# Products of the scan states with C for three of four chunks on GpSimd, sums and gates of the finished chunk three steps later

## What is computed

```python
def _L0_attn_ref(u, in_proj_w, dt_projs_weight, dt_projs_bias, x_proj_w, A, D, norm_B_w, norm_C_w, out_proj_w):
    xz = u @ in_proj_w.T
    x, z = jnp.split(xz, 2, axis=-1)
    x = jax.nn.silu(x)
    dt = jax.nn.softplus(x @ dt_projs_weight.T + dt_projs_bias)
    BCp = (x @ x_proj_w.T).reshape(Bsz, L, NHEADS, -1)
    ...
    Bc = jax.lax.complex(Bn[..., 0], Bn[..., 1])
    Cc = jax.lax.complex(Cn[..., 0], Cn[..., 1])
    ...
    zt = Ac[None, None] * (0.5 * dt)[..., None]
    den = 1.0 - zt
    abar = (1.0 + zt) / den
    u_in = Bc * ((dt * x_sum)[..., None] / den)
    def step(h, inp):
        a, b = inp
        h = a * h + b
        return (h, h)
    _, hs = jax.lax.scan(step, h0, (jnp.swapaxes(abar, 0, 1), jnp.swapaxes(u_in, 0, 1)))
    y_red = jnp.real(Cc * hs).sum(axis=-1)
    y = (xh * (y_red + D)[..., None]).reshape(Bsz, L, D_INNER)
    y = y * jax.nn.silu(z)
    return y @ out_proj_w.T
```

## Time and profile before

| | |
|---|---|
| median of 3 runs | 1005.39 us (1004.13 to 1006.34) |
| the profiled execution | 1000.66 us |
| its span, first to last instruction | 998.3 us |
| mean granted TensorE clock | 0.919 of full speed |
| PE busy | 814.4 us (82%) |
| DVE busy | 737.3 us (74%) |
| ACT busy | 560.7 us (56%) |
| POOL busy | 200.5 us (20%) |
| scan on VectorE, first to last step | 290.6 to 534.7 us |

### The profile page before, as it was taken

One profiled execution on the slowest core, in us unless ns is written; L12 is line 12 of the kernel. 1 busy time (PEld: TensorE's weight loads), 2 busy tenths in 40 slices (PEclk: granted clock), 3 DMA queues, 4 the chain that ended last, 5 costly groups with the idle time before them and its releaser, 6 DMA issues. The chain is left out here.

```text
span 998.3 us, 26552 instructions
## 1 busy us (share of the span) xinstructions
PE 814.4 (82%) x9663; PEld 482.8 (48%) x9663; DVE 737.3 (74%) x2440; ACT 560.7 (56%) x1410; POOL 200.5 (20%) x216
## 2 busy tenths in 40 slices
PE   4899999998865788696683387796996999999787
PEld 2577777775322233242231264564665555555453
DVE  5688888885589999999996885456563666666667
ACT  3689888988674658566240576454433333333345
POOL 1477666764000000000000011002110000000037
PEclk9999999999997788998796698998797999999979
DMA  7111111100000000000000702100570000000001
GB/s 247 34 45 40 42 37 42 37 16 3 1 0 1 1 0 1 1 1 0 1 0 1 177 2 98 75 4 3 197 298 14 1 1 0 0 0 0 2 9 34
DMA packets 23415, 36.56 MB, mean 37 GB/s; under 512 B 5668, under 2 KB 19748, under 8 KB 21156
## 3 DMA queue, kind: packets, MB, share of 16 engines
q1 hardware_dynamic: 23336, 35.53, 11.3%
HBM read 34.48 MB, written 1.05 MB: 36 GB/s over the span
## 5 line engine op out<-in xcount | busy, mean ns | idle before, releaser
L442 ACT ACTIVATE xa_prob<-xa_s,xa_nmax 128x257 f32<-128x257 f32 x256 | 128.1, 503 | 21.0 <-DVE xa_nmax L579 19.3
L726 POOL TENSOR_TENSOR xa_prob<-xa_prob,xa_rinv 128x1028 f32<-128x1028 f32 x64 | 121.5, 1900 | 76.7 <-DVE xa_rinv L586 75.7
L579 DVE CUSTOM_DVE_ANT_0 xa_s<-xa_s_ps,xa_nbias 128x257 f32<-128x257 f32 x256 | 93.2, 420 | 12.3 <-ACT xa_prob L442 6.4
L1637 POOL TENSOR_TENSOR mo_disp_t<-mo_disp_t,mo_rst 128x256 f32<-128x256 f32 x16 | 9.8, 615 | 362.3 <-DVE mo_rst L1616 362.3
L2262 PEld LDWEIGHTS ca_z_ps<-ca_xn_t,ca_m_t 128*128 128x128 f32 x512 | 62.1, 199 | 30.5 <-issue 25.9
L2345 ACT COPY ca_z<-ca_z_ps 128x512 f32<-128x512 f32 x64 | 37.5, 585 | 69.0 <-PE ca_z_ps L2262 69.0
L272 PE MATMUL xa_t_ps<-identity,xa_prob 128*128 128x128 f32 x512 | 69.5, 279 | 4.1 <-ACT xa_p_t L451 1.8
L2262 PE MATMUL ca_z_ps<-ca_xn_t,ca_m_t 128*128 128x128 f32 x512 | 67.9, 288 | 4.0 <-ACT ca_xn_t L2339 3.9
L569 DVE COPY xa_kvs<-xa_kv_ps 128x512 f32<-128x512 f32 x64 | 44.1, 689 | 34.3 <-PE xa_kv_ps L246 34.3
L272 PEld LDWEIGHTS xa_t_ps<-identity,xa_prob 128*128 128x128 f32 x512 | 54.8, 141 | 25.6 <-issue 25.6
L451 ACT COPY xa_p_t<-xa_t_ps 128x1024 f32<-128x1024 f32 x64 | 63.4, 991 | 2.2 <-PE xa_t_ps L272 2.2
(11 more groups left out here) (353 smaller groups left out, 1912.6 us busy)
## 6 DMA issues: line engine op xcount, KB each, us to landing
xa_ctx_t<-in_ctx_t SPq DMA_DIRECT2D x64, 128.5 KB, 2.1
room<-in_ctx_t SPq DMA_DIRECT2D x8, 1028.0 KB, 6.5
room<-in_ctx_n SPq DMA_DIRECT2D x8, 1024.0 KB, 4.8
ss_wx<-in_ss_wx SPq DMA_DIRECT2D x1, 2048.0 KB, 7.9
xres<-in_x SPq DMA_DIRECT2D x4, 256.0 KB, 5.3
out_x<-xres SPq DMA_DIRECT2D x4, 256.0 KB, 2.3
ma_mask_u<-in_mask SPq DMA_DIRECT2D x4, 128.5 KB
room<-in_ca_wk SPq DMA_DIRECT2D x1, 512.0 KB, 3.5
```

The source lines that it names most:

```text
L442: nc.scalar.activation(prob[:, r, g, :], s_sb[:, b, g, :], ACT.Exp, bias=nmax[:, r, g:g + 1], scale=-1.0, accum_out=rsum[:, r, g:g + 1]).t ...
L579: nc.vector.tensor_tensor_reduce(out=s_sb[:, b, g, :], in0=s_ps[:, g, 0:S], in1=nbias[:, g, :], scale=1.0, scalar=3e38, op0=ALU.add, op1=A ...
L726: nc.gpsimd.tensor_tensor(prob[:, r, :, :], prob[:, r, :, :], bc(rinv[:, r, :].rearrange("p (g o) -> p g o", o=1), (P, G, S)), ALU.mult).t ...
```

## The change

For chunks 0, 1 and 2 the four products of the states with C are taken from VectorE's table and given to GpSimd, as a block of its own with the same operands. The first product of a chunk waits until the last step of the chunk is done, each waits for its C planes, and nothing stands between them. The products of chunk 3 stay on VectorE. `scaled_y`, `gated_y`, `residual`, the row statistics, the moments and (in chunks 1 and 2) the decay work move later: from (6,1) to (9,1), from 8 and 9 to 11 and 12, from 13 to 16, from 14 and 18 to 17 and 21, and from 14, 16, 19, 21 to 16, 18, 21, 23. `step_size` and `input_size` move earlier, from step 9 to step 7. On TensorE `reduce_y(c - 1)` goes behind `step_sizes(c + 1)`.

```diff
@@ state_space, tensor @@
-                if c >= 1:
-                    reduce_y(c - 1)
                 if more:
                     step_sizes(c + 1)
                 if c >= 1:
+                    reduce_y(c - 1)
                     spread_y(c - 1)
@@ state_space, vector, fill(c, l, gap) @@
-                if before and gap < 2 and 1 <= l < 3:
-                    outputs(c - 1, 2 * (l - 1) + gap)
...
-                if before and at == (6, 1):
+                if before and at == (9, 1):
                     scaled_y(c - 1)
-                if before and gap == 1 and l in (8, 9):
-                    gated_y(c - 1, l - 8)
-                if after and at == (9, 0):
+                if before and gap == 1 and l in (11, 12):
+                    gated_y(c - 1, l - 11)
+                if after and at == (7, 0):
                     step_size(c + 1)
-                if after and at == (9, 2):
+                if after and at == (7, 2):
                     input_size(c + 1)
-                if before and at == (13, 1):
+                if before and at == (16, 1):
                     residual(c - 1)
...
-                first = (14, 16, 19, 21) if before else (18, 20, 23, 25)
+                first = (16, 18, 21, 23) if before else (18, 20, 23, 25)
@@ state_space, new @@
+        @block.gpsimd
+        def _(pool):
+            def outputs(c, h):
+                if h == 0:
+                    pool.wait_ge(step_done, (5 * N - 1) * (c + 1))
+                pool.wait_ge(c_ready, 8 * c + 2 * h + 2)
+                nc.gpsimd.tensor_tensor(w[:, c % 2, :, h, :], w[:, c % 2, :, h, :], c_pl[:, :, h, :], ALU.mult).then_inc(prod_ready, 1)
+
+            for c in range(CH - 1):
+                for h in range(H):
+                    outputs(c, h)
```

8 lines of the change are left out of this document (4 added, 4 removed).

## The result

The new kernel takes 1020.39 us (median of 4 runs, 1018.49 to 1021.37) against 1004.76 us of the kernel before on the same chip (4 runs, 1000.13 to 1006.34). The ratio is 1.016 [1.012, 1.020]. The forecast was 1019.8 us. Run a second time later, the new kernel had 1.0185 [1.0151, 1.0218].

What follows compares the result with a forecast made beforehand. VectorE was taken to bound the scan, busy 63.03 of 66.20 us in chunk 1. 24.6 us of standstill, less 12.1 of products and 1.7 of old waits, plus 3.6 of newton waits, gave +14.4 us: 1019.8 us, range 1009 to 1028 us.

Steps and rivals of the forecast that it cites:

- GpSimd's product: Duration of one 1024-element product on GpSimd, 2.35 us from its other rows; four take 9.4 us.
- The standstill: VectorE's scan instructions held by GpSimd's products at the start of chunks 1 to 3: 8.2 us each, 24.6 us together.
- The products taken off VectorE: Four products fewer in each of three chunks, 1.01 us each: 4.04 us a chunk, 12.1 us saved.
- the old waits: VectorE's waits at L1236 just ahead of (9,0) go: 1.10 us in chunk 1, 0.6 us in chunk 2.
- The step size: In (7,0) VectorE arrives 2.1 us after the softplus and does not wait; undisturbed it would wait 6.1 us in chunk 1.
- The newton: In (16,0) VectorE waits 1.8 us in chunks 1 and 2, as spread_y runs at TensorE's lower clock after idleness.
- The scan in all: Sum over chunks 1 to 3: 24.6 us less 12.1 and 1.7 us, plus 3.6 us, +14.4 us.
- Chunk 0 and all later stages keep their length: Sign to check: everything outside chunks 1 to 3, the work behind the scan included, stays unchanged in length.
- no standstill: Rival: GpSimd's reads go beside the scan's without holding VectorE; 1003.2 us, or 1006.8 us with newton waits; 8%.
- the partial one: Rival: GpSimd gives way while running, VectorE loses 3 to 5.5 us per chunk; 1007.2 to 1010.8 us; 15%.
- the heavier one: Rival: VectorE's instructions lengthen GpSimd's or get in less often, 11 us per chunk; 1028 us; 11%.

Runs made afterwards that it cites:

- other tiles: Kernel before, products on VectorE, plus four unused 1024-element GpSimd TENSOR_TENSORs at the start of chunks 1 to 3 on tiles of their own: 1019.7 us, ratio 1.016.
- quarters: Changed kernel with each GpSimd product cut into four pieces, sixteen for a chunk: 1017.31 us, ratio 1.017.
- the kernel with TensorE kept busy: Changed kernel with seven extra 512-column matmuls, result overwritten, ahead of spread_y's wait on TensorE: 1010.81 us, ratio 1.011.
- the seven matmuls: Changed kernel with seven extra matmuls ahead of spread_y's wait, 512 columns wide (1010.81 us, ratio 1.011) or one column wide (1013.1 us, ratio 1.011).
- thirteen short matmuls: Kernel before with gates one step later and thirteen one-column matmuls ahead of the last reduce_y's wait for the products: 993.6 us, ratio 0.991.
- Kept busy ahead: Kernel before with gates one step later and thirteen 512-column matmuls ahead of the last reduce_y's wait for the products: 994.7 us, ratio 0.994.
- the moves only: Changed kernel with its twelve products put back on VectorE at (1,0) to (2,1), all other moves kept: 1006.3 us, ratio 1.004.
- GpSimd only: Kernel before with only the products of chunks 0 to 2 given to GpSimd, all else in its old place: 1012.86 us, ratio 1.009.

## Why the prediction was right, point by point

The median came out 0.6 us above the forecast. The scan did what the forecast says, for the reasons that it gives. One stage that was to keep its length grew, and the fit of the totals is partly luck.

- **GpSimd's product**, taken from the slope of its rows as 2.35 us: 2.355 to 2.401 us. Right.
- **The standstill**, 8.2 us for a chunk by the rule "one VectorE instruction gets in for each GpSimd instruction": 8.36 us. Right, and the mechanism was shown twice more: with other tiles (it follows GpSimd's reads, not the data) and with quarters (it follows the number of pieces). One row that the forecast leaned on is of another kind: L2082 is a TENSOR_SCALAR with one large input, and no run here tests that kind.
- **The products taken off VectorE**, 1.01 us each, and the old waits, 1.7 us. Chunk 3, with nothing else in it, came out +4.3 against 8.2 - 4.04 = +4.2 us. In the changed kernel all waits at L1235 are behind the scan, so the 1.7 us went as written. On their own they would not have gone in full: with the gates one step later only 1.0 us came off, since the step size was late next. The standstill covers that too.
- **The step size** in (7,0) waits for nothing. Right, and right for the given reason: without the standstill it waits 2.8 us in the two chunks together.
- **The newton**, 1.8 us in each of chunks 1 and 2 from a TensorE at its lower clock: 1.38 and 1.62 us. L948 took 3.78 us where I had 3.48. Shown by the kernel with TensorE kept busy: its two waits vanish and chunks 1 and 2 are 1.7 and 2.1 us shorter.
- **The scan in all**: +14.4 us forecast, +14.6 us measured, chunk by chunk 4.9, 5.4, 4.2 against 4.7, 5.6, 4.3. The 0.2 us are closer than the parts: the standstill was 0.5 us too low in all and the newton 0.6 us too high, and the second trace of the new kernel has +13.8 us.
- **"Chunk 0 and all later stages keep their length"** is the step that failed. The tail grew by 3.4 us, because L948 and L955 behind the scan ran at the lower clock too. I had read the granted clock at the place where the change leaves TensorE idle, and not asked what level it has in the work after the scan, though the changed kernel shifts the idle time ahead of that as well: 11.76 us between L930 and L939 instead of 17.56 us. In before the clock was back at its upper level 3.4 us after L939 began, ahead of L948. In the changed kernel it came back 12.5 us after, at 567.90 us, when L955 was nearly done, although TensorE was busy for 10.9 of these 12.5 us. In four traces with idle times of 11.76 to 11.90 us there (the change twice, and with either kind of the seven matmuls) L948 took 3.78 us; in nine with 10.61 to 17.56 us it took 1.98 or 1.99 us, the 10.61 us being those with thirteen short matmuls just ahead. Kept busy ahead, TensorE ran it at 3.78 us too, after 2.21 us. The length of the idle time alone does not order them, so what sets the moment at which the clock is given back stays open. Neither half of the change lengthens the tail by itself: it has 15.2 us with the moves only and 14.8 us with GpSimd only.
- **Span against median.** The spans differ by 18.4 us, the medians by 15.6. The profiled execution of before lay 4.1 us under its median and that of after 0.7 us; a second trace of the new kernel had a span of 1012.8 us. Of the 3.4 us of the tail the medians therefore show no more than a part. Against the kernel before, the medians show +15.6 us and, the second time, 1019.47 - 1002.31 = +17.2 us, where +14.4 us was forecast. So the forecast was 1 to 3 us too low, about the size of the tail, and that 1019.8 and 1020.4 us fit to 0.6 us is luck: the median of 1005.39 us, on which it stands, came out at 1004.76 us with a fourth run.

Of the rivals, "no standstill" and the partial one fall with the first five rows of chunk 1; the heavier one, in which VectorE gets in less often, falls with the same rows.

## What to carry to other kernels

Before moving work from VectorE to GpSimd, look at what VectorE does beside it. In a dense row of instructions with two operands in SBUF each GpSimd instruction that reads costs VectorE its own duration less one short instruction, here 2.09 us, twice the 1.01 us that the product had cost in place. Where VectorE's work beside it is of another kind, such as L2573 with its large input from PSUM, that price is not due. Before moving a reader later in TensorE's queue, price its matmuls at the lower clock: the idle time that the move opens can halve their speed (1.88 us became 3.78), and whoever is behind them gets the difference. Ask the same of the matmuls after the stage. And look for "issue" rows on TensorE far from the edit: a few one-column matmuls more took 3 to 6 us off the experts' stage here (0.991 against 0.998 of the time before, with the gates one step later in both), which was more than any order of the scan brought, and the kernel with both is the one to keep.
